# 16-head attention: the first head's turn placed behind the keys, its values between two queries, and the query norms between the last turn and its values

## The reference, cut to what matters

```python
q = rmsnorm((hidden_states @ Wq).reshape(B, Sq, H, D), gq)
k = rmsnorm((encoder_hidden_states @ Wk).reshape(B, Skv, H, D), gk)
v = (encoder_hidden_states @ Wv).reshape(B, Skv, H, D)
scores = jnp.einsum('bqhd,bkhd->bhqk', q, k) * scale
attn = jax.nn.softmax(scores, axis=-1)
out = jnp.einsum('bhqk,bkhd->bqhd', attn, v).reshape(B, Sq, H * D)
return out @ Wo
```

## Time and profile before

| | |
|---|---|
| time of the runs (3) | 3647.87 us median, 3645.5 to 3652.24 |
| profiled execution | 3656.33 us, of it the span of the core 3654.6 us |
| mean granted clock of TensorE | 0.944 of full speed |
| PE busy | 3205.6 us (88%) |
| PE weight loads busy | 1927.0 us (53%) |
| DVE busy | 2597.2 us (71%) |
| ACT busy | 1805.8 us (49%) |
| POOL busy | 1401.3 us (38%) |
| stage of the change | about 1529 to 2935 us of the span, units 0 to 14 in 1574 to 2861 |

### The profile page before, as it was taken

How to read it: one execution, slowest core, us unless ns; L and a number is a source line. 1 busy time by engine, 2 the same in 40 slices (tenths; PEclk the granted TensorE clock), 3 DMA queues, 4 the chain that set the end, 5 groups by cost and what they waited for, 6 DMA issues and landing times. The chain is left out here.

```text
span 3654.6 us, 43452 instructions
## 1 busy us (share of the span) xinstructions
PE 3205.6 (88%) x14597; PEld 1927.0 (53%) x14628; DVE 2597.2 (71%) x3488; ACT 1805.8 (49%) x3413; POOL 1401.3 (38%) x956
## 2 busy tenths in 40 slices
PE   5849888899997788799999999999999888997996
PEld 2327745333333455465555555555555456785763
DVE  5853678787774888567777777777777755665786
ACT  4544434466564444465555566655565332664220
POOL 1022168200000000065666667766666644223540
PEclk9878899899999999999999999999999898998998
DMA  2125646222225400144545445544444346665321
GB/s 92 48 105 210 252 159 153 69 64 55 57 45 129 75 1 1 70 146 163 164 153 164 153 164 171 167 149 167 156 154 151 106 171 206 228 249 209 138 69 58
DMA packets 229736, 478.70 MB, mean 131 GB/s; under 512 B 36224, under 2 KB 69632, under 8 KB 213649
## 3 DMA queue, kind: packets, MB, share of 16 engines
q1 hardware_dynamic: 223280, 459.19, 39.2%
q0 software_dynamic: 6240, 16.81, 1.3%
HBM read 387.51 MB, written 92.06 MB: 131 GB/s over the span
## 5 line engine op out<-in xcount | busy, mean ns | idle before, releaser
L2306 POOL TENSOR_TENSOR l2x_inflow<-l2x_dtu,l2x_rows_b 128x512 f32<-128x512 f32 x256 | 432.2, 1688 | 330.5 <-DVE l2x_state L2195 308.5
L178 POOL TENSOR_TENSOR ln_work<-ln_work,minus_half 128x4 f32<-128x4 f32 (+1 forms) x34 | 33.2, 978 | 1048.6 <-DVE ln_work L166 1048.5
L2195 DVE TENSOR_TENSOR_SCAN l2x_state<-l2x_decay,l2x_inflow 128x512 f32<-128x512 f32 x256 | 385.0, 1504 | 17.0 <-ACT l2x_decay L2069 17.0
L1265 DVE TENSOR_REDUCE l1x_mx<-psum 128x2 f32<-128x1024 f32 x256 | 308.2, 1219 | 100.4 <-PE psum L1107 99.0
L2009 ACT ACTIVATE l2x_probs<-psum,l2x_soft,l2x_norms 128x512 f32<-128x512 f32 x256 | 195.7, 775 | 319.1 <-DVE l2x_soft L2133 319.1
L2322 POOL TENSOR_TENSOR l2x_y_sum<-l2x_y_sum,l2x_state 128x512 f32<-128x512 f32 x224 | 340.6, 1521 | 33.0 <-DVE l2x_state L2204 33.0
L1222 ACT ACTIVATE l1x_split<-psum 128x1024 f32<-128x1024 f32 x256 | 262.2, 1025 | 158.9 <-PE psum L1107 158.8
L126 PE MATMUL psum<-l2x_probs_t,l2x_v_tok 128*128 128x512 f32 x512 | 239.4, 611 | 32.1 <-ACT l2x_probs_t L212 26.0
L2204 DVE TENSOR_TENSOR l2x_state<-l2x_state,l2x_rows_c 128x512 f32<-128x512 f32 x256 | 252.1, 985 | 6.5
L126 PE MATMUL psum<-l2x_xt,l2x_wq 128*128 128x512 f32 x512 | 231.0, 595 | 7.8 <-issue 6.3
L126 PE MATMUL psum<-l2x_kt,l2x_qt 128*128 128x512 f32 x512 | 230.5, 593 | 4.0 <-ACT l2x_probs L2009 4.0
(11 more groups left out here) (440 smaller groups left out, 7336.7 us busy)
## 6 DMA issues: line engine op xcount, KB each, us to landing
l2x_rows_b<-l3x_xd_dram SPq DMA_DIRECT2D x256, 256.0 KB, 3.6
l2x_rows_c<-l3x_xd_dram SPq DMA_DIRECT2D x256, 256.0 KB, 3.5
l2w_raw<-l_w SPq DMA_DIRECT2D x38, 1024.0 KB, 7.0
l2x_wkv<-l2x_kv_dram SPq DMA_DIRECT2D x32, 1024.0 KB, 6.9
l2w_raw<-l_w SPq DMA_DIRECT2D x38, 512.0 KB
l1x_heads_dram<-l1x_stage SPq DMA_DIRECT2D x32, 512.0 KB, 3.3
l2x_wq<-l_wq SPq DMA_DIRECT2D x16, 1024.0 KB, 7.0
l2x_wo<-l_wo SPq DMA_DIRECT2D x16, 1024.0 KB, 5.4
```

Source lines behind the costliest of these rows:

```text
L1265: main.drain(dve.tensor_reduce(mx[:, gg % 2, :, j, t], g["psum"][:, b:b + 2, :], AX.X, ALU.max), f"m{n}_0", banks=2)
L2195: dve.tensor_tensor_scan(state[:, s % KEPT, :], decay[:, s % 3, :], inflow[:, s % 3, :], 0.0, ALU.mult, ALU.add).then_inc(scan_done, 1)
L2306: pool.tensor_tensor(inflow[:, s % 3, :], dtu[:], rows_b[:, s % 3, :], ALU.mult).then_inc(inflow_ready, 1)
```

## The change

On PE, turn(u, 0) moves from behind query(u + 1, 0) to ahead of score(u, 1), and value(u, 0) from behind query(u + 1, 1) to ahead of it; query_norms(u + 1) moves from ahead of turn(u, 3) to behind it. The ring's list follows. On ACT, turn(u, 0) moves ahead of exponent(u, 1), with one decay between them, and inverse(u, 0) ahead of query(u + 1, 1). On DVE, query_norms(u + 1) moves behind turn(u, 3). POOL and SP stay as they were.

```diff
--- before.py
+++ after.py
@@ -1753,10 +1753,10 @@
         if (u + 1) % G2 == 0 and pre:
             jobs += [(f"xt{(u + 1) // G2}_{c}", "act" if c % 2 else "dve") for c in range(DC)]
         jobs += [(f"k{u + 1}_{t}", "act") for t in range(ST)] if pre else []
-        jobs += score(1) + query(0) + turn(0) + query(1) + value(0) + turn(1) + score(2) + value(1) + query(2)
-        jobs += turn(2) + score(3) + query(3) + value(2)
+        jobs += turn(0) + score(1) + query(0) + value(0) + query(1) + turn(1) + score(2) + value(1) + query(2)
+        jobs += turn(2) + score(3) + query(3) + value(2) + turn(3)
         jobs += [(f"ssq{u + 1}", "dve")] if pre else []
-        jobs += turn(3) + value(3)
+        jobs += value(3)
         jobs += [(f"v{u + 1}_{t}", "act") for t in range(ST)] if pre else []
         jobs += [(f"kt{u + 1}_{h}", "dve") for h in range(4)] if pre else []
         jobs += [(f"out{u}_{t}", "dve") for t in range(ST)] if on else []
@@ -1977,11 +1977,11 @@
                 x_turned(u + 1)
                 context(u + 1, "k", (0, 1))
                 context(u + 1, "k", (2, 3))
+                turn(u, 0)
                 score(u, 1)
                 query(u + 1, 0)
-                turn(u, 0)
+                value(u, 0)
                 query(u + 1, 1)
-                value(u, 0)
                 turn(u, 1)
                 score(u, 2)
                 value(u, 1)
@@ -1990,8 +1990,8 @@
                 score(u, 3)
                 query(u + 1, 3)
                 value(u, 2)
+                turn(u, 3)
                 query_norms(u + 1)
-                turn(u, 3)
                 value(u, 3)
                 context(u + 1, "v", range(ST))
                 keys_turned(u + 1)
@@ -2076,14 +2076,14 @@
                 decays(u, 1)
                 context(u + 1, "k", k_tok)
                 decays(u, 2)
+                turn(u, 0)
+                decays(u, 3)
                 exponent(u, 1)
-                decays(u, 3)
                 query(u + 1, 0)
                 decays(u, 4)
-                turn(u, 0)
+                inverse(u, 0)
                 query(u + 1, 1)
                 decays(u, 5)
-                inverse(u, 0)
                 key_scale(u + 1, 0)
                 decays(u, 6)
                 turn(u, 1)
```

## The result

The changed kernel takes 3668.48 us (median of 4; 3667.44 to 3671.57) where the kernel before took 3649.65 on the same chips (four runs, the three shown above and one more, with the median over all four): a ratio of 1.0053, with a 95% interval of 1.0038 to 1.0067. It is slower by 18.8 us; the forecast was 16 us slower. The profiled execution took 3667.45 us.

What follows compares the result with a forecast made beforehand. TensorE was taken to set the pace, busy 1243 of 1287 us. Terms of +1.4 and -0.3 us over 15 units gave +16.5 us, against the median of 3647.87 a forecast of 3664 us, range 3638 to 3683.

Steps and rivals of the forecast that it cites:

- The bank waits of head 1's scores: TensorE, head 1's score tiles: waits for banks of ACT's k copies replace the 1.65 us gap, +0.35 us at turn 1.
- The walk: Unit 5 traced in the new order, in the old trace's clock: turn 2 at 2043.6 against 2042.18.
- DVE late, a bank held, turn 2 +1.4: DVE's value product of head 0 comes 2.65 us late, holding head 2's third score tile: +1.4 us a unit.
- The bias: DVE's bias behind head 2's maxima, 1.15 us in the old run, was taken as short without GpSimd's inflow.
- rival 3: Head 2's exponentials hold turn 2 as the bias stays 1.15 us: +2.1 us a unit, 3679 us; chance 0.19.
- Second edit, -0.3: Turn 3 ahead of the query norms: value 2 to v context takes 10.4 us, not 10.69, lower clock in 13 of 15.
- the first edit: Head 0's turn moved behind the keys: +1.4 us a unit, bounds +0.35 and +2.4.
- The sum: Over 15 units, +1.4 and -0.3 us each: +16.5 us, giving 3664 us; chance 0.40.
- The last unit: Unit without k context, carried by DVE's scans: counted as 0, between -4 and +1 us.
- DVE catching up: DVE's lateness is eaten between 2024 and 2034: +0.4 us a unit, 3654 us, no change; chance 0.20.
- The clock no longer falling: Values 3 keep the full clock behind the norms: -1.1 us a unit, 3631 us; chance 0.18.
- The shared port: DVE's scans 3 and 4 wait for GpSimd's key-norm power: 0.5 us a unit later, 3671 us; chance 0.03.

Runs made afterwards that it cites:

- The experiment with scan 3 ahead: The changed kernel with DVE's scan 3 and gather 3 moved ahead of head 1's maxima and biases: 3661.01 us, ratio 1.0029.
- the late reciprocal: The changed kernel with DVE's reciprocal of head 1 moved from behind scan 4 to behind head 0's value product: 3668.93 us, ratio 1.0054.
- the kernel with both DVE moves: The changed kernel with scan 3 and gather 3 ahead of head 1's maxima, and head 1's reciprocal behind head 0's value product: 3660.16 us, ratio 1.0020.
- Alone, the edit: The kernel before with only turn 3 moved ahead of the query norms: 3642.51 us, ratio 0.9977.
- The run of the first edit alone: The changed kernel with the query norms put back ahead of turn 3 on PE, DVE and in the ring's list: 3679.45 us, ratio 1.0073.

## Why the prediction was right

**The bank waits of head 1's scores.** The walk put query 0 at 2019.3, that is 16.9 us into the unit: measured 16.9. Turn 1 +0.35: measured +0.5.

**DVE late, a bank held, turn 2 +1.4.** The product was to come 2.65 us late; it came 2.25 late, the third score tile waited for it as stated, and turn 2 was 1.24 us late. The experiment with scan 3 ahead took that wait away and some 8 us of the 18.8 with it (3661.0 against the 3668.9 of the late reciprocal on the same chip). What is left, turn 2 0.8 us late, goes with the bank waits of head 1's scores and ACT's copies of turn 1, as the kernel with both DVE moves shows. But the step that leads to DVE's lateness was named wrongly: the prediction has "DVE's reciprocal for head 1 waits for those exponentials". Moved away, the reciprocal changed nothing. The binding wait was one step earlier, DVE's maxima that now meet score tiles 1.66 us apart, with scan 3 behind them; my walk had written the tiles' times down and had not taken them over to DVE. Scan 4, which the walk let run in 1.22 us, took 2.29. With these the reciprocal came where the walk had it (2024.4 in the old clock, against 2024.5), so that the number stood is luck.

**The bias.** Taken as short, measured 0.16 us; rival 3, which needed 1.15, falls in this kernel. (In the kernel with both DVE moves it was 1.17 and turn 2 did not come later.)

**Second edit, -0.3.** The size of one fall is right (10.4 against 8.8, 1.6 us where I took 1.5), the stretch at full clock was put at 9.1 and is 8.7 to 8.8, since the values run only 3.0 us up to the context, not 3.4. What was wrong is the number of falls: I carried over 13 in 15. Alone, the edit had 10 with a fall; in the kernel after 14 stretches had one, three of them for twice as long. The edit's own term is -0.7 a unit, not -0.3, with the first edit and without it. The number of falls could not be read off another kernel's trace: the sums are 160.36, 170.70, 159.70 and 149.50 us in four kernels.

**The term that was missing.** The prediction costs the first edit by what it does up to turn 2 and puts its effect on the clock behind the norms at nothing. The run of the first edit alone shows +0.7 us a unit there.

**The sum.** +1.1 a unit: +1.15 up to turn 3 (1.23 to 1.24 in fourteen units, 0.1 in the first) and -0.04 behind it. By the edits, the first costs +1.15 and +0.7 where I had +1.4, and the second -0.7 where I had -0.3. Two errors of some 0.4 us cancel, so that the sum came out so near is luck; the bank waits and the late value product are not. The last unit, counted as 0 with +1 at most, took 1.6 more; the wait of 6.23 us there is the same wait of head 2's scores for DVE's value product.

**The rivals.** DVE catching up: no, 2.25 of 2.65 us arrived. The clock no longer falling: in one unit, not ten. The shared port: with scan 3 at 2018.48 and GpSimd's power at its key norms from 2016.48 on for 2.9 us, the scan took 1.23 us (in all 15 units 1.22 or 1.23), so, as in the earlier trace rows, the pair does not exclude each other for the whole instruction; the Trainium skill, "SBUF — State Buffer", section "Who interferes with whom", would have the scan wait until 2019.4.

## What to carry to other kernels

When an early step is moved ahead on one engine, follow its evictions on the engine that makes them: here the turn was free on TensorE, but ACT had to finish the keys first, and everything behind the turn's copies moved back. Count the ring's banks for each job whose predecessor changes, and carry each new arrival time to every engine that reads the tile, in-order queues included. Where a clock reacts to what the engine did, an order that saves some tenths can lose as much through where its gaps fall, so such a gain is to be confirmed by more than one arrangement.

## What the hardware showed unexpectedly

Waiting of TensorE cost more in one piece: three pieces of 0.54 us between products left the granted clock at 1.00, one gap of 3.06 us was followed by a stretch at the lower level in which query 0's four products took 5.2 us instead of 3.4. It was so in seven units of seven, but gaps of 3.3 and 3.73 us elsewhere were once each followed by the full clock. Products with 32 columns take as long as products with one (3.5 us for the same 16), and the clock fell less often behind them. And a GpSimd power on a tile of 16 columns, 2.9 to 3.8 us long, did not hold up DVE's scans (1.22 and 1.23 us), while its products on 512 columns did (2.29 us). The power itself took 2.9 us where no scan was running at its start, and 3.7 to 3.8 where it began 0.15 to 0.26 us behind the start of one.
